# Image planes stored as 16 x 8 cells on 128 partitions, tokens by band, in a four-layer convolution kernel on one core

## The chip, the cores and the metric

One core of a Trainium2 chip runs the whole kernel in one launch. The metric is the device time of one execution in microseconds (us).

## The reference

The input is an image of 256 x 256 pixels with 128 channels, in fp32. Four layers follow each other: attention over rows, a Fourier layer with a feed-forward part, a layer of 1-D convolutions, and a gated 7 x 7 depthwise convolution. The change touches the last two. With x2 the input of the third layer, v and p its convolved values:

```
layer 3:  x3 = x2 + shift + q            (q: two ReLU'd pointwise products, added and shifted by columns)
layer 4:  n  = group_norm(x3)            (one scale and shift per channel, from statistics over the image)
          b  = conv7x7(n, B_kernel),  g = conv7x7(n, gate_B_kernel)      (per channel, periodic edges)
          bt = b * sigmoid(g)
          out = x3 + softplus(bt)-like hidden state @ W_out + b_out
```

At the 49 pixels around the origin a second kernel (A_kernel) acts as well, so those pixels are computed anew at the end.

## The kernel before, in words

The image is cut into patches of 8 x 8 pixels (PATCH); a row of patches has PX = 32 of them, and two rows of patches, 16 image rows, are a band (BAND). The stages that matter run one after another, with a barrier of all engines between them. Nearly every DMA is issued by SP, in the order written in its program; each engine works its own list in order and waits on semaphores.

**pointwise_part** (from L1301) makes x3. It has 128 tiles of two image rows, channels on partitions. A step t of the loop does, on PE, the product p_v (L1437) of tile t+1 and p_r (L1443) of tile t; on ACT, v (L1465) and r (L1477); on DVE, p (L1498), z (L1511) and, of the tile before, x3b (L1520, one instruction per image row); on POOL, q (L1415 to L1418). When a band of eight tiles is complete, it goes out in eight chunks e, nine steps after its tile: PE turns four patch columns (L1450) so that the 128 pixels of a patch column and band lie on partitions, ACT copies the result twice, into x3n (L1471) and into plane (L1481), and DVE takes statistics (L1528). SP stores x3n to the DRAM tensor x3t (L1389; "tokens"), from two buffers: ACT's copy of chunk e waits for the store of chunk e-2. After the eighth chunk POOL copies the edge columns of plane (L1423, L1424), and SP stores it to the DRAM tensor planes, in the pieces that pieces(g) lists: a band is shifted by HALO = 3 rows against the patches, so these are runs of 5, 8 and 3 rows (L1395).

```
tokens = x3t.rearrange("(g y) d a c -> g (y d) (a c)", y=BAND)
act.wait_ge(tokens_stored[e % 2], 16 * (e // 2))
```

**patch_weights** (from L1544) builds the convolution as matrices: for each group of 4 channels a [112, 2, 4, 128] block that maps a window of 14 columns x 8 rows (112 partitions, WROWS), in two halves, to 64 pixels of both convolutions. It ends with two DMAs that store them to patch_w (L1577).

**depthwise_layer** (from L1627) is the convolution and what follows it. A block b is four rows of patches; there are 8 blocks of 16 units each, 128 units u. In a unit PE turns eight slices (L1749), does two conv groups g (L1737; each 4 channels x 2 halves, reading a window and a block of weights) and one projection w = u - 6 (L1760). ACT and DVE evaluate gate and softplus (L1795 to L1813; L1857 to L1872), DVE adds the residual to the output (L1880), POOL adds a bias to the residual (L1839). Conv runs 34 groups (lead) ahead of the first turn. SP's program for unit u is: the windows of pair k = u + 17 (three DMAs, L1683), the weights of its two groups (L1689), the residual of w = u - 5 (L1695), and the four output stores of w = u - 8 (L1702), one for each image row:

```
sp.dma_start(out[0, r * PATCH + y + i].rearrange("(a d) c -> d a c", d=PATCH)[x:x + 4],
             outs[:, w % 3, i]).then_inc(stored[w % 3], 16)
```

Before them it waits: windows for the conv three pairs back, weights for the conv four groups back, the residual for `added` of w - 3, and the store for `added` of its own w.

**origin_patch** (from L1897) loads the surroundings of the origin in 27 small DMAs (L1943), and computes its 49 pixels.

## Time and profile before

| | us |
|---|---|
| median of three runs | 7585.48 (7583.73 to 7593.19) |
| the profiled execution | 7594.39 |
| its span, first to last instruction | 7592.7 |
| attention, Fourier layer and all before 4880 us | 4880, PE busy 4671 |
| pointwise stage with the statistics' end, 5080 to 5980 | 900 |
| patch weights, 5980 to 6154 | 174 |
| depthwise stage, 6154 to 7527 | 1373 |
| origin patch, 7527 to 7593 | 66 |

The profile is that of one execution. Busy is the time in which an engine executed an instruction; the DMA share is the mean over the 16 DMA engines of the core of the time in which they moved packets; GB/s is what all of them moved; PEclk is the granted TensorE clock as a share of 2.4 GHz. A wait is idle time of an engine ahead of an instruction, put down to what ended it.

### The profile page before, as it was taken

How to read it: one execution, taken by the hardware profiler on the slowest of the kernel's cores; microseconds unless marked ns; L12 is line 12 of the kernel's file. 1: busy time of each engine (PE TensorE's matmuls, PEld its weight loads, DVE VectorE, ACT ScalarE, POOL GpSimd, SP SyncE). 2: the span in 40 equal slices, each digit the busy share in tenths (PEclk: the TensorE clock that was granted, in tenths of full speed). 3: DMA queues.
4: the chain of work that ended last, by engine and by line, in shares of the span. 5: the costliest groups of instructions: out<-in, count | busy, mean ns of one | idle time of the engine just before them, and what ended most of it. 6: DMA issues, size and time to landing. Idle time of an engine off the chain costs nothing. (4 is left out here: it accounts for less than half of the span.)

```text
span 7592.7 us, 110044 instructions
## 1 busy us (share of the span) xinstructions
PE 6234.0 (82%) x29856; PEld 4091.6 (54%) x29856; DVE 3902.4 (51%) x11300; ACT 3821.1 (50%) x9727; POOL 569.5 (8%) x879
## 2 busy tenths in 40 slices
PE   7999999999999999977999899854444557777763
PEld 5777777777777776424444344311111347766663
DVE  7777777777777777413333333224444203333335
ACT  3777777777777776223444444433333203333333
POOL 0000000000000000001000000013333000111111
PEclk9999999999999999999999999987777568888886
DMA  5111111111111111673111111355444189888882
GB/s 200 34 35 35 35 34 35 35 34 34 35 35 35 34 35 41 211 230 96 59 61 56 62 59 61 107 187 164 161 156 157 52 204 207 196 195 199 196 197 70
DMA packets 759166, 773.64 MB, mean 102 GB/s; under 512 B 52640, under 2 KB 631769, under 8 KB 748121
## 3 DMA queue, kind: packets, MB, share of 16 engines
q1 hardware_dynamic: 738986, 719.10, 33.9%
q0 software_dynamic: 13312, 41.96, 1.4%
q10 hardware_dynamic: 6720, 10.76, 0.4%
q8 instruction: 75, 1.23, 0.1%
q14 instruction: 73, 0.60, 0.0%
HBM read 566.01 MB, written 205.61 MB: 102 GB/s over the span
## 5 line engine op out<-in xcount | busy, mean ns | idle before, releaser
L428 ACT ACTIVATE at_probs<-at_neg_s,at_neg_max 128x256 f32<-128x256 f32 x2048 | 1018.0, 499 | 327.1 <-DVE at_neg_max L480 320.6
L359 PE MATMUL at_p_s<-at_keys,at_qz 128*128 128x256 f32 x4096 | 1107.0, 393 | 3.2 <-ACT at_qz L453 2.5
L480 DVE CUSTOM_DVE_ANT_0 at_neg_s<-at_p_s,at_bias 128x256 f32<-128x256 f32 x2048 | 782.2, 419 | 592.7 <-PE at_p_s L359 592.6
L1737 PE MATMUL dw_p_conv<-dw_xw,dw_wts 112*128 112x128 f32 x4096 | 643.6, 323 | 412.5 <-issue 349.1
L1737 PEld LDWEIGHTS dw_p_conv<-dw_xw,dw_wts 112*128 112x128 f32 x4096 | 609.8, 235 | 433.7 <-issue 432.9
L359 PEld LDWEIGHTS at_p_s<-at_keys,at_qz 128*128 128x128 f32 x4096 | 697.7, 190 | 267.4 <-issue 209.1
L347 PE MATMUL at_p_o<-at_probs_t,at_vs 128*32 128x256 f32 x4096 | 810.0, 385 | 0.0
L492 DVE TENSOR_SCALAR at_probs<-at_probs,at_inv 128x256 f32<-128x256 f32 x2048 | 631.0, 351 | 36.2
L339 PE MATMUL at_p_t<-all_ident,at_probs 128*128 128x128 f32 x4096 | 587.1, 276 | 1.6 <-DVE at_probs_t L471 1.6
L1443 PE MATMUL pw_p_r<-pw_p,pw_w 128*128 128x512 f32 x256 | 170.4, 753 | 459.8 <-DVE pw_p L1498 459.6
L339 PEld LDWEIGHTS at_p_t<-all_ident,at_probs 128*128 128x128 f32 x4096 | 466.8, 141 | 133.1 <-issue 105.9
L1795 ACT ACTIVATE dw_gate<-dw_p_turn,dw_f_shift,dw_nscale 128x512 f32<-128x512 f32 x128 | 99.4, 777 | 792.2 <-PE dw_p_turn L1749 792.2
L935 PE MATMUL ml_p<-ml_h,l_w 128*128 128x512 f32 x1024 | 485.0, 597 | 1.6 <-DVE ml_h L1002 1.6
L347 PEld LDWEIGHTS at_p_o<-at_probs_t,at_vs 128*32 128x32 f32 x4096 | 284.7, 109 | 368.2 <-issue 128.2
L951 PE MATMUL ml_p<-ml_h,l_w1s 128*128 128x512 f32 x1024 | 469.2, 601 | 1.3 <-DVE ml_normed L1010 1.3
L1872 DVE SCALAR_TENSOR_TENSOR dw_hid<-dw_bt,dw_soft 128x512 f32<-128x512 f32 x128 | 135.2, 1057 | 592.5 <-ACT dw_soft L1813 592.5
L422 ACT ACTIVATE at_probs_t<-at_p_t 128x512 f32<-128x512 f32 x512 | 305.9, 597 | 249.6 <-PE at_p_t L339 243.3
L453 ACT ACTIVATE at_qz<-at_p_qk 32x256 f32<-32x256 f32 x1024 | 384.3, 375 | 92.0 <-PE at_p_qk L405 82.9
L981 ACT ACTIVATE ml_h<-ml_p,l_b 128x512 f32<-128x512 f32 x384 | 248.0, 679 | 282.6 <-PE ml_p L935 282.6
L428 ACT ACTIVATION_READ_ACCUMULATOR at_probs<-at_neg_s,at_neg_max 128x1 f32 x2048 | 386.2, 189 | 0.0
L1443 PEld LDWEIGHTS pw_p_r<-pw_p,pw_w 128*128 128x128 f32 x256 | 49.0, 226 | 567.5 <-DVE pw_p L1498 547.0
L471 DVE COPY at_probs_t<-at_p_t 128x512 f32<-128x512 f32 x512 | 349.3, 682 | 0.5 <-PE at_p_t L339 0.5
(214 smaller groups left out, 9837.9 us busy)
## 6 DMA issues: line engine op xcount, KB each, us to landing
dw_wts<-patch_w SPq DMA_DIRECT2D x256, 448.0 KB, 8.2
sp_xs<-x SPq DMA_DIRECT2D x256, 256.0 KB, 3.2
dw_xw<-planes SPq DMA_DIRECT2D x128, 337.5 KB
in_xs<-in_x_dram SPq DMA_DIRECT2D x32, 1024.0 KB
at_xs<-in_x_dram SPq DMA_DIRECT2D x256, 128.0 KB, 2.1
at_kvs<-in_L_conv_kv_x_dram SPq DMA_DIRECT2D x256, 128.0 KB, 2.3
x<-at_x1s SPq DMA_DIRECT2D x256, 128.0 KB, 1.9
ml_xs<-x SPq DMA_DIRECT2D x128, 256.0 KB
```

Of the source, the lines that this page charges most:

```text
L339: mm = pe.transpose(p_t[h % 2][:, kh, qh * 128:(qh + 1) * 128], probs[:, h, qh, kh * 128:(kh + 1) * 128], ident[:, :])
L347: mm = pe.matmul(p_o[ch, 0, :], vs[:, row.r % 2, kh, ch], probs_t[:, h, kh, :], start=kh == 0, stop=kh == HALVES - 1)
L359: mm = pe.matmul(p_s[h % 2][:, qh, :], qz[:, row.r % 2, h, qh * 128:(qh + 1) * 128], keys[:, row.r, h // 2, :], start=True, stop=True)
L422: act.activation(probs_t[:, h], p_t[h % 2][:, :, :], ACT.Copy).then_inc(odd_read, 1)
L428: e = act.activation(probs[:, h, qh, :], neg_s[:, h % 2, qh, :], ACT.Exp, bias=neg_max[:, row.r % 2, i:i + 1], scale=-1.0, accum_out=sums[ ...
L453: t = act.activation(qz[ch, two.r % 2, h, :], p_qk[ch, 0, :], ACT.Copy, scale=float(HEAD_DIM) ** -0.5)
L471: dve.tensor_copy(probs_t[:, h], p_t[h % 2][:, :, :]).then_inc(even_read, 1)
L480: t = dve.tensor_tensor_reduce(neg_s[:, h % 2, qh, :], p_s[h % 2][:, qh, :], bias[:, h, qh, :], -1.0, 3.0e38, ALU.add, ALU.min, neg_max[:, ...
L492: t = dve.tensor_scalar(probs[:, h, qh, :], probs[:, h, qh, :], inv[:, p, j:j + 1], None, ALU.mult)
L935: pe.matmul(p_1[b][:, :], w0[:, b * 128:(b + 1) * 128], h[:, :], start=True, stop=True).then_inc(hid_made, 1)
L951: mm = pe.matmul(p_2[:, :], w1c[:, b, :], h1[:, b, :], start=b == 0, stop=b == blocks - 1)
L1737: mm = pe.matmul(p_conv[g % 2][:, j, :], wts[:, g % 4, half, j, :], xw[:, k % 3, half:half + BLOCK_PY, g % 2 * 4 + j, 0:PX], start=half == ...
```

## The change

The planes are kept as cells of 16 rows x 8 columns: the DRAM tensor planes has 264 image rows, 8 columns d, 128 channels and 33 patch columns (WIDE), shifted by four columns (SHIFT), so that a window is 128 partitions of one DMA and the second half of a window is the next patch column (side) instead of the next patch row. The weights have 128 partitions. x3b gets a 33rd column of patches and is written in four instructions per tile instead of two; POOL copies its first column's edge (x3_wrapped), and PE and DVE wait for that. x3t is ordered by band, patch column, pixel of the band. Tokens have four buffers; the planes of a band go out in eight DMAs, one a step, from 18 steps behind the tile, with an edge DMA in the first and in the last band. In the depthwise stage residual and output are four DMAs each of 32 partitions x 4 rows; they have four buffers, the residual is loaded one unit later and the output stored two units later in SP's order.

```diff
-WIDE = PX + 2
-PATCH_ROWS = ROWS // PATCH + 1
+WIDE = PX + 1
+SHIFT = PATCH // 2
...
-    tokens = x3t.rearrange("(g y) d a c -> g (y d) (a c)", y=BAND)
+    tokens = x3t[:, :, 0:128].rearrange("g a p c -> g p a c")
...
-        x3b = m.sb("x3b", [128, 2, PX, BAND, PATCH])
-        x3n = m.sb("x3n", [128, 2, 4, CH])
+        x3b = m.sb("x3b", [128, 2, PX + 1, BAND, PATCH])
+        x3n = m.sb("x3n", [128, 4, 4, CH])
...
-        tokens_stored = [m.sem(f"tokens_stored{i}") for i in range(2)]
+        tokens_stored = [m.sem(f"tokens_stored{i}") for i in range(4)]
...
-        steps = range(-2, tiles + 12)
...
+        steps = range(-2, tiles + 20)
+        bands = ROWS // BAND
+        edge = SHIFT * PATCH
+        first_row = planes[0:SHIFT].rearrange("y d c a -> (y d) (c a)")
+        last_row = planes[ROWS + SHIFT:ROWS + 2 * SHIFT].rearrange("y d c a -> (y d) (c a)")
+        body = planes[SHIFT:ROWS + SHIFT].rearrange("(g y) d c a -> g (y d) (c a)", y=BAND)
+        part = CH * WIDE // 8
+
+        def token_stores(e):
+
+            return 16 * (e // 4) + (16 * len(range(0, e, 8)) if e % 4 == 0 else 0)
 
         def plane_stores(parity, g):
 
-            return 16 * sum(len(pieces(k)) for k in range(parity, g, 2))
+            return 16 * 8 * len(range(parity, g, 2)) + (16 if parity == 0 and g > 0 else 0) + (16 if g == bands and parity else 0)
 
         @block.sync
...
-                    sp.dma_start(tokens[e // 8][:, e % 8 * 4 * CH:(e % 8 + 1) * 4 * CH],
-                                 x3n[:, e % 2].rearrange("p a c -> p (a c)")).then_inc(tokens_stored[e % 2], 16)
-                if e >= 0 and e % 8 == 7:
-                    g = e // 8
-                    sp.wait_ge(plane_wrapped, g + 1)
-                    for y, n, r_at, y_at in pieces(g):
-                        sp.dma_start(planes[r_at, :, y_at:y_at + n].rearrange("d y c a -> y d (c a)"),
-                                     plane[y * PATCH:(y + n) * PATCH, g % 2].rearrange("p c a -> p (c a)")
-                                     ).then_inc(planes_stored[g % 2], 16)
+                    sp.dma_start(tokens[e // 8][:, e % 8 * 4:(e % 8 + 1) * 4], x3n[:, e % 4]).then_inc(tokens_stored[e % 4], 16)
+                    if e % 8 == 0:
+                        sp.dma_start(tokens[e // 8][:, PX], x3n[:, 0, 0]).then_inc(tokens_stored[0], 16)
+                f = t - 18
+                if 0 <= f < chunks:
+                    g, k = f // 8, f % 8
+                    flat = plane[:, g % 2].rearrange("p c a -> p (c a)")
+                    if k == 0:
+                        sp.wait_ge(plane_wrapped, g + 1)
+                    sp.dma_start(body[g][:, k * part:(k + 1) * part], flat[:, k * part:(k + 1) * part]
+                                 ).then_inc(planes_stored[g % 2], 16)
+                    if k == 7 and g == 0:
+                        sp.dma_start(last_row, flat[0:edge]).then_inc(planes_stored[0], 16)
+                    if k == 7 and g == bands - 1:
+                        sp.dma_start(first_row, flat[128 - edge:128]).then_inc(planes_stored[1], 16)
+            for s in range(4):
+                sp.wait_ge(tokens_stored[s], token_stores(chunks + s))
             for s in range(2):
-                sp.wait_ge(tokens_stored[s], 16 * (chunks // 2))
-                sp.wait_ge(planes_stored[s], plane_stores(s, ROWS // BAND))
+                sp.wait_ge(planes_stored[s], plane_stores(s, bands))
...
+                if 0 <= t - 8 < tiles and t % 8 == 0:
+                    g = t // 8 - 1
+                    pool.wait_ge(x3_made, 8 * g + 8)
+                    pool.tensor_copy(x3b[:, g % 2, 0, :, 0:SHIFT], x3b[:, g % 2, PX, :, 0:SHIFT]).then_inc(x3_wrapped, 1)
...
-                    pool.tensor_copy(plane[:, g % 2, :, 0:1], plane[:, g % 2, :, PX:PX + 1])
-                    pool.tensor_copy(plane[:, g % 2, :, PX + 1:PX + 2], plane[:, g % 2, :, 1:2]).then_inc(plane_wrapped, 1)
+                    pool.tensor_copy(plane[:, g % 2, :, PX:PX + 1], plane[:, g % 2, :, 0:1]).then_inc(plane_wrapped, 1)
...
                     pe.wait_ge(x3_made, 8 * g + 8)
+                    pe.wait_ge(x3_wrapped, g + 1)
...
-                    if e >= 2:
-                        act.wait_ge(tokens_stored[e % 2], 16 * (e // 2))
-                    act.activation(x3n[:, e % 2], p_n[e % 2][:, :, :], ACT.Copy).then_inc(tokens_read, 1)
+                    if e >= 4:
+                        act.wait_ge(tokens_stored[e % 4], token_stores(e))
+                    act.activation(x3n[:, e % 4], p_n[e % 2][:, :, :], ACT.Copy).then_inc(tokens_read, 1)
...
-                    act.activation(plane[:, g % 2, :, 1 + px:5 + px], p_n[e % 2][:, :, :].rearrange("p a c -> p c a"),
+                    act.activation(plane[:, g % 2, :, px:px + 4], p_n[e % 2][:, :, :].rearrange("p a c -> p c a"),
                                    ACT.Copy).then_inc(plane_read, 1)
...
                     for i in range(2):
-                        x3 = dve.scalar_tensor_tensor(out=x3b[:, g % 2, :, y + i, :],
-                                                      in0=xs[:, y + 1 + i].rearrange("p (a d) -> p a d", d=PATCH), scalar=shift,
-                                                      in1=q[:, s, i].rearrange("p (a d) -> p a d", d=PATCH),
-                                                      op0=ALU.add, op1=ALU.add)
+                        for d, a_at in ((0, 1), (SHIFT, 0)):
+                            cols = slice(SHIFT - d, 2 * SHIFT - d)
+                            x3 = dve.scalar_tensor_tensor(
+                                out=x3b[:, g % 2, a_at:a_at + PX, y + i, d:d + SHIFT],
+                                in0=xs[:, y + 1 + i].rearrange("p (a d) -> p a d", d=PATCH)[:, :, cols], scalar=shift,
+                                in1=q[:, s, i].rearrange("p (a d) -> p a d", d=PATCH)[:, :, cols], op0=ALU.add, op1=ALU.add)
                     x3.then_inc(x3_made, 1)
...
                     dve.wait_ge(x3_made, 8 * g + 8)
+                    dve.wait_ge(x3_wrapped, g + 1)
...
-        sel = m.sb("sel", [KTAPS, 2 * PATCH, PATCH - 1 + WINDOW, PATCH])
+        sel = m.sb("sel", [KTAPS, BAND, PATCH - 1 + BAND, PATCH])
         kt = m.sb("kt", [KTAPS, 2, CH])
-        tw = m.sb("tw", [WROWS, 2, CH, 2 * SPOTS])
+        tw = m.sb("tw", [128, 2, CH, 2 * SPOTS])
...
                     mm = pe.matmul(p_w[n % 4][:, i].rearrange("p f c -> p (f c)"),
-                                   sel[:, first, PATCH - 1 - ox:PATCH - 1 - ox + WINDOW, :].rearrange("t a b -> t (a b)"),
+                                   sel[:, half * PATCH - ox + PATCH - 1, PATCH - 1 - oy:PATCH - 1 - oy + BAND, :].rearrange("t a b -> t (a b)"),
                                    kt[:, :, :].rearrange("p f c -> p (f c)"), start=True, stop=True)
...
-        xw = m.sb("xw", [WROWS, 3, BLOCK_PY + 1, 8, WIDE])
-        wts = m.sb("wts", [WROWS, 4, 2, 4, 2 * SPOTS])
+        xw = m.sb("xw", [128, 3, BLOCK_PY, 8, WIDE])
+        wts = m.sb("wts", [128, 4, 2, 4, 2 * SPOTS])
...
-        xr = m.sb("xr", [128, 3, 4, CH])
-        outs = m.sb("outs", [128, 3, 4, CH])
+        xr = m.sb("xr", [128, 4, 4, CH])
+        outs = m.sb("outs", [128, 4, 4, CH])
...
         flat = xw[:, :, :, :, :].rearrange("p k r c a -> p k r (c a)")
-        run = 8 * WIDE - 2
+        run = 8 * WIDE
         cell = CH * WIDE
 
-        def field(r, d, y, c, col, planes_of):
-
-            at = ((r * PATCH + d) * PATCH + y) * cell + c * WIDE + col
-            return bass.AP(planes.tensor, at, [[cell, planes_of * PATCH], [PATCH * PATCH * cell, BLOCK_PY + 1], [1, run]])
+        def windows(b, c):
+
+            at = b * BLOCK_PY * PATCH * PATCH * cell + c * WIDE
+            return bass.AP(planes.tensor, at, [[cell, 128], [PATCH * PATCH * cell, BLOCK_PY], [1, run]])
...
-                for d, n, at, col in ((PATCH - HALO, HALO, 0, 0), (0, PATCH, HALO, 1), (0, HALO, HALO + PATCH, 2)):
-                    sp.dma_start(flat[at * PATCH:(at + n) * PATCH, k % 3, :, 0:run],
-                                 field(b * BLOCK_PY, d, 0, c, col, n)).then_inc(x_loaded[k % 3], 16)
+                sp.dma_start(flat[:, k % 3], windows(b, c)).then_inc(x_loaded[k % 3], 16)
...
             def load_residual(w):
-                r, x, y = w // 4, w // 2 % 2 * 4, w % 2 * 4
-                if w >= 3:
-                    sp.wait_ge(added, w - 2)
-                sp.dma_start(xr[:, w % 3],
-                             x3t[r * PATCH + y:r * PATCH + y + 4, x:x + 4].rearrange("y d a c -> (d a) y c")).then_inc(r_loaded[w % 3], 16)
+                r, x, y = w // 4, w // 2 % 2, w % 2 * 4
+                if w >= 4:
+                    sp.wait_ge(added, w - 3)
+                cells = x3t[r // 2, x:x + PX, r % 2 * 64:r % 2 * 64 + 64].rearrange("a (y d) c -> d a y c", d=PATCH)
+                for d in range(4):
+                    sp.dma_start(xr[d * PX:(d + 1) * PX, w % 4], cells[(1 - x) * SHIFT + d][:, y:y + 4]).then_inc(r_loaded[w % 4], 16)
 
             def store(w):
                 r, x, y = w // 4, w // 2 % 2 * 4, w % 2 * 4
                 sp.wait_ge(added, w + 1)
-                for i in range(4):
-                    sp.dma_start(out[0, r * PATCH + y + i].rearrange("(a d) c -> d a c", d=PATCH)[x:x + 4],
-                                 outs[:, w % 3, i]).then_inc(stored[w % 3], 16)
+                for d in range(4):
+                    sp.dma_start(out[0, r * PATCH + y:r * PATCH + y + 4].rearrange("y (a d) c -> d a y c", d=PATCH)[x + d],
+                                 outs[d * PX:(d + 1) * PX, w % 4]).then_inc(stored[w % 4], 16)
...
-                if 0 <= u - 5 < total:
-                    load_residual(u - 5)
-                if 0 <= u - 8 < total:
-                    store(u - 8)
-            for s in range(3):
-                sp.wait_ge(stored[s], 64 * ((total - s + 2) // 3))
+                if 0 <= u - 6 < total:
+                    load_residual(u - 6)
+                if 0 <= u - 10 < total:
+                    store(u - 10)
+            for s in range(4):
+                sp.wait_ge(stored[s], 64 * (total // 4))
...
-                    pe.wait_ge(x_loaded[k % 3], 48 * (k // 3 + 1))
+                    pe.wait_ge(x_loaded[k % 3], 16 * (k // 3 + 1))
...
-                    for half in range(2):
-                        mm = pe.matmul(p_conv[g % 2][:, j, :], wts[:, g % 4, half, j, :],
-                                       xw[:, k % 3, half:half + BLOCK_PY, g % 2 * 4 + j, 0:PX],
-                                       start=half == 0, stop=half == 1)
+                    for side in range(2):
+                        mm = pe.matmul(p_conv[g % 2][:, j, :], wts[:, g % 4, side, j, :],
+                                       xw[:, k % 3, :, g % 2 * 4 + j, side:side + PX], start=side == 0, stop=side == 1)
...
-                pool.wait_ge(r_loaded[w % 3], 16 * (w // 3 + 1))
-                pool.tensor_tensor(xr[:, w % 3], xr[:, w % 3], b_plain.unsqueeze(1).broadcast_to((128, 4, CH)),
+                pool.wait_ge(r_loaded[w % 4], 64 * (w // 4 + 1))
+                pool.tensor_tensor(xr[:, w % 4], xr[:, w % 4], b_plain.unsqueeze(1).broadcast_to((128, 4, CH)),
...
-                if w >= 3:
-                    dve.wait_ge(stored[w % 3], 64 * (w // 3))
-                dve.tensor_tensor(outs[:, w % 3], p_out[w % 2][:, :, :], xr[:, w % 3], ALU.add).then_inc(added, 1)
+                if w >= 4:
+                    dve.wait_ge(stored[w % 4], 64 * (w // 4))
+                dve.tensor_tensor(outs[:, w % 4], p_out[w % 2][:, :, :], xr[:, w % 4], ALU.add).then_inc(added, 1)
...
-                k = min(left, 128 - at % 128)
-                pieces.append((at, y, x, k))
+                k = min(left, 128 - at % 128, PATCH - (x + SHIFT) % PATCH)
+                pieces.append((at, y, x + SHIFT, k))
...
+        def cells(y, x, k):
+
+            first = y % BAND * PATCH + x % PATCH
+            return x3t[y // BAND, x // PATCH, first:first + k]
...
-                sp.dma_start(xs[at % 128:at % 128 + k, at // 128, :], x3t[y, x % PATCH:x % PATCH + k, x // PATCH]).then_inc(loaded, 16)
+                sp.dma_start(xs[at % 128:at % 128 + k, at // 128, :], cells(y, x, k)).then_inc(loaded, 16)
...
-    x3t = scratch("x3t", [ROWS, PATCH, PX, CH])
-    planes = scratch("planes", [PATCH_ROWS, PATCH, PATCH, CH, WIDE])
+    x3t = scratch("x3t", [ROWS // BAND, WIDE, BAND * PATCH + 1, CH])
+    planes = scratch("planes", [ROWS + 2 * SHIFT, PATCH, CH, WIDE])
```

## Rows read from the trace of the kernel before

**Rows 1.** Busy by stage: us, each engine, granted clock, DMA share, GB/s
```profile
5080.00:5980.00 900.00, 372.01 (x1030) 168.29 (x1030) 408.59 (x648) 299.30 (x513) 288.97 (x544) 0.73 0.47 155
6300.00:7500.00 1200.00, 850.82 (x5446) 831.48 (x5447) 437.79 (x608) 422.37 (x738) 159.19 (x124) 0.82 0.82 190
```

**Rows 2.** Waits, 5090 to 5940 us: total, times, longest
```profile
DVE pw_x3b L1520 <- POOL pw_q L1418: 421.2, 80, 28.9
ACT pw_x3n L1471 <- DMA x3t<-pw_x3n: 371.7, 16, 29.3
```

**Rows 3.** Busy by short stretch, columns as in rows 1
```profile
5916.00:5933.00 17.00, 0.00 (x0) 0.00 (x0) 0.28 (x1) 0.00 (x0) 0.00 (x0) 0.50 0.34 125
7522.00:7526.00 4.00, 0.00 (x0) 0.00 (x0) 0.00 (x0) 0.00 (x0) 0.00 (x0) 0.50 0.25 75
6180.00:6270.00 90.00, 68.33 (x430) 66.05 (x430) 9.68 (x14) 7.77 (x13) 0.00 (x0) 0.77 1.02 221
20.00:60.00 40.00, 31.17 (x256) 27.48 (x254) 38.91 (x65) 0.00 (x0) 0.00 (x0) 1.00 1.01 415
3250.00:3350.00 100.00, 84.62 (x188) 18.58 (x186) 0.00 (x0) 28.18 (x48) 0.00 (x0) 1.00 0.83 267
```

**Rows 4.** Timeline, 5360 to 5385 us: start, us, engine, line
```profile
5361.59 0.88 DVE L1520 SCALAR_TENSOR_TENSOR pw_x3b<-pw_xs,all_coef,pw_q 128x256 f32<-128x256 f32 x2 [2.28 <-POOL pw_q L1418]
...
5363.58 1.66 DVE L1511 SCALAR_TENSOR_TENSOR pw_z<-pw_xs,all_coef,pw_taus 128x512 f32<-128x512 f32 x1
...
5376.48 1.17 DVE L1520 SCALAR_TENSOR_TENSOR pw_x3b<-pw_xs,all_coef,pw_q 128x256 f32<-128x256 f32 x2
```

**Rows 5.** Timeline, end of the pointwise stage
```profile
5934.74 0.60 ACT L1471 ACTIVATE pw_x3n<-pw_p_n 128x512 f32<-128x512 f32 x1 [20.34 <-DMA x3t<-pw_x3n]
...
5944.77 6.01 SPq L1395 DMA_DIRECT2D planes<-pw_plane  x4
5973.85 3.62 DVE L173 BATCH_NORM_AGGREGATE l_gn_mv<-stats 128x2 f32<-128x768 f32 x1 [57.58 <-PEq L77]
```

**Rows 6.** Tile pw_xs: ns min/median/max, first and last start
```profile
L1520 DVE SCALAR_TENSOR_TENSOR pw_x3b<-pw_xs,all_coef,pw_q x256: 471/483/1462, 5093.5 to 5910.3; 128x256 f32<-128x256 f32 x128
```

**Rows 7.** DMA issues, 6400 to 7500 us: KB each, us to landing
```profile
dw_wts<-patch_w SPq DMA_DIRECT2D x192, 448.0 KB, 8.2
dw_xw<-planes SPq DMA_DIRECT2D x96, 337.5 KB
...
dw_xr<-x3t SPq DMA_DIRECT2D x115, 256.0 KB, 7.2
dw_xw<-planes SPq DMA_DIRECT2D x192, 126.6 KB
```

**Rows 8.** Tile dw_p_turn: ns min/median/max, first and last start
```profile
L1749 PE MATMUL dw_p_turn<-all_ident,dw_raw x1024: 273/310/421, 6280.1 to 7489.2; 128*128 128x128 f32 x171
```

**Rows 9.** Timeline, one unit of the depthwise stage
```profile
6805.07 5.52 SPq L1702 DMA_DIRECT2D out_dram<-dw_outs  x4
...
6809.72 2.02 PE L1737 MATMUL dw_p_conv<-dw_xw,dw_wts 112*128 112x128 f32 x16 [2.04 <-issue]
...
6811.58 1.05 PE L1760 MATMUL dw_p_out<-all_w_plain,dw_hid 128*128 128x128 f32 x8
...
6814.26 1.33 PE L1749 MATMUL dw_p_turn<-all_ident,dw_raw 128*128 128x128 f32 x8
```

**Rows 10.** Busy in two stretches, columns as in rows 1
```profile
6500.00:6700.00 200.00, 143.20 (x927) 140.14 (x926) 67.88 (x97) 65.14 (x114) 24.66 (x19) 0.83 0.85 197
4880.00:5028.00 148.00, 116.72 (x258) 20.98 (x258) 0.34 (x2) 62.67 (x32) 0.00 (x0) 0.97 0.70 242
```

**Rows 11.** Timeline, the store of the patch weights and the next stage
```profile
6100.00 15.12 SPq L1577 DMA_DIRECT2D patch_w<-kw_tw  x2
6154.36 1.04 SPq L1683 DMA_DIRECT2D dw_xw<-planes  x2
```

**Rows 12.** Tile og_xs: ns min/median/max, first and last start
```profile
L1943 SPq DMA_DIRECT2D og_xs<-x3t x27: 258/296/300, 7527.3 to 7536.1; - x27
```

More of the change, by code:

```diff
@@ L1534 @@
 SPOTS = PATCH * PATCH
-WROWS = PATCH * WINDOW
 BLOCK_PY = 4
@@ L1559, in patch_weights @@
         p_t = m.ps("p_t", [KTAPS, 2, CH])
-        p_w = [m.ps(f"p_w{i}", [WROWS, 2, 2, CH]) for i in range(4)]
+        p_w = [m.ps(f"p_w{i}", [128, 2, 2, CH]) for i in range(4)]
         p_b = m.ps("p_b", [128, CH])
@@ L1658, in depthwise_layer @@
         w_loaded = [m.sem(f"w_loaded{i}") for i in range(4)]
-        r_loaded = [m.sem(f"r_loaded{i}") for i in range(3)]
-        stored = [m.sem(f"stored{i}") for i in range(3)]
+        r_loaded = [m.sem(f"r_loaded{i}") for i in range(4)]
+        stored = [m.sem(f"stored{i}") for i in range(4)]
         scaled, prepared, biased = m.sem("scaled"), m.sem("prepared"), m.sem("biased")
@@ L1712, in _ @@
                 load_weights(2 * k + 1)
-            for u in range(total + 8):
+            for u in range(total + 10):
                 k = u + lead // 2
@@ L2075, in build @@
     tau = scratch("tau", [TOKENS])
-    patch_w = scratch("patch_w", [CH // 4, WROWS, 2, 4, 2 * SPOTS])
+    patch_w = scratch("patch_w", [CH // 4, 128, 2, 4, 2 * SPOTS])
     with ExitStack() as ctx:
```

29 lines of the change are left out of this document (7 added, 22 removed).

## The prediction

> **What bounds the kernel now.** I read the busy shares by stage first, then the waits, then short stretches with only one kind of transfer in flight, then timelines of one tile and one unit.
>
> The pointwise stage lasts 900 us, and no engine is busy for half of it: DVE 409, PE 372, ACT 299 us [rows 1]. The waits give the reason: ACT stands 371.7 us in 16 waits, one per band, for the token store to leave its buffer [rows 2], 23.2 us each. DVE's 421 us behind POOL's q is the same wait further down the chain. During such a wait (5916 to 5933) the DMA share is 0.34 at 125 GB/s [rows 3]: transfers are outstanding, yet two thirds of the DMA engines rest. What is outstanding is a burst: the band's planes go out in DMAs of 5, 8 and 3 rows (680, 1088, 408 KB), 17,408 bytes to a packet, and the token stores queue behind them. At the stage's end the burst runs alone, from its issue at 5944.8 to the next stage's first work at 5973.9 [rows 5].
>
> The depthwise stage is about 1370 us. Per unit PE does 48 matmul records (32 conv, 8 turn, 8 project); 927 in 200 us [rows 10] are 19.3 units, so a unit takes 10.35 us. I use 10.3. PE is busy 72% of it, at clock 0.83, and its idle time stands before the first conv of a unit (2.04 us in this one [rows 9]), with no releaser but its loads. SP spends 5.52 us on the four output stores [rows 9], though an issue costs 0.52 us (two in 1.04 [rows 11]); the rest is waiting for room in the queue. When only stores are left (7522 to 7526) the DMA share is 0.25 at 75 GB/s [rows 3]: a store occupies four engines of sixteen. Those four are the bound. A unit moves 591 KB windows, 896 KB weights and 256 KB each of residual and of output (four stores of 64 KB) [rows 7]. Windows and weights, 1.52 MB at the 221 GB/s of the lead phase (share 1.02 [rows 3]), take 6.9 us; 0.26 MB of output at 75 GB/s takes 3.5 us on four engines; the sum, 10.4, is a unit.
>
> The Trainium skill (DMA: Bandwidth & Descriptors, section "Why a DMA increments its semaphore by 16 and not by 1") says that a DMA runs on the largest number of engines up to 16 that divides the slowest dimension of both sides. By it the old output stores (DRAM side 4 x 32) run on 4, the plane pieces on 5, 8 and 3, the old side windows (24 partitions) on 12, and every new form of these on 16. The trace agrees for the stores (share 0.25); for the other forms no row isolates it.
>
> **Pointwise stage, part by part.** The plane burst becomes eight DMAs per band, one per tile, each over 128 partitions with 2,112 bytes, issued a band later. Tokens get four buffers instead of two. So nothing large stands ahead of a token store, and I take all 16 waits away. Next late is DVE. Between waits, x3 starts at 5361.59 and four tiles later at 5376.48 [rows 4]: 3.72 us per tile.
>
> Added: x3 is made by four instructions of 128 elements instead of two of 256. A 512-element one takes 0.74 us [rows 4], a 256-element one 0.48 [rows 6], so 128 elements are some 0.35 us: 4 x 0.35 - 2 x 0.48 = +0.44 us, less the overlap that makes a pair 0.88 [rows 4]; I take +0.33. Below: 0, since DVE also waits here for POOL (2.28 us [rows 4]); above: 2 x 0.48 = +0.97. So 4.05 us per tile, bounds 3.7 and 4.7. From 5093.5 to 5910.3 [rows 6], 817 us, it becomes 127 x 4.05 = 514: **-303 us** (-347 to -220).
>
> At nothing: the new POOL copy of x3's edge, once a band (one plane copy goes, and POOL is busy 289 of 900 us); PE and DVE's wait for it comes a tile later; the token store's 512 packets of 512 bytes in place of 128 of 2,048, with the same bytes. A tile moves 1.07 MB. At the 267 GB/s and share 0.83 of a stretch with loads and stores together [rows 3], that is 322 GB/s at full share and 3.3 us, below 4.05. If that cover went, 221 GB/s would give 4.8 us per tile (+95 us). SP issues four or five DMAs a tile, 2.1 to 2.6 us at 0.52. ACT's wait for planes two bands back now ends with a part issued in the same step; the step's length covers it, or it costs up to 2 us in 14 bands.
>
> The end: from the last x3 at 5910.3 to 5973.9 is 63.5 us, 20.3 of it a token wait and 29 the last burst [rows 5]. Then: eight chunks at about 1.2 us, 10; the POOL copy, 1; 2.2 MB of planes and the 0.5 MB edge at 322 GB/s, 8; landing and step lags, 5. Together 24: **-39 us**.
>
> **Patch weights.** 112 partitions become 128: bytes +14%. The store takes 54.4 us from issue to the next stage [rows 11]: +7.8 at the same rate; at 415 GB/s the 16.8 MB are 40 us, -14. The first row is nearer; I take **+3 us**. Matmuls move as many columns as before.
>
> **Depthwise stage.** Windows: one DMA of 528 KB for three; weights 1024 KB for 896. The lead phase loads 17 pairs between its first load at 6154.4 [rows 11], plus 8 us to land, and the first turn at 6280.1 [rows 8]: 118 us, 6.9 us each. 1.59 MB at 322 GB/s are 4.9 us, at 221 7.2. I take 5.1: **-31 us** (-45 to +5).
>
> A unit then moves 2.11 MB on all engines: 6.6 us at 322, 5.1 at 415, 9.6 at 221 GB/s. I take 322, since that row mixes loads and stores as a unit does. PE needs 2 x 2.02 + 1.05 + 1.33 = 6.4 us [rows 9]; a stretch busy for 79% was granted 0.97 [rows 10], so 6.6. Two limits of 6.6 us that don't stay in step give some 0.7 us on top: 7.3, bounds 6.5 and 8.0. DVE (68 us in 19.3 units) and ACT (65) need 3.5. SP issues 11 DMAs instead of 10, 5.7 us at 0.52. For 110 units: 3.0 x 110 = **-330 us**.
>
> That the new stores and residual loads use all engines is a choice between two rows: the form with 4 outermost on the DRAM side ran at share 0.25, the loads with 24 to 128 outermost at share 1.0 [rows 3]; the new ones have 32 outermost on both sides. The moved store: it now waits for an output three steps old, so SP does not stand there, and the next unit's windows and weights behind it in SP's queue are not held. The residual load comes one unit later; it is needed about two units (15 us) on, against 7.2 us to landing [rows 7] and POOL's 1.3. If that cover went, DVE would wait with its next raw copy behind it. The last 17 units have no loads and run on the ACT-DVE chain: 0 (-10 to +5).
>
> **Origin patch.** 53 load DMAs instead of 27. 27 take 8.8 us in a row [rows 12], 0.34 each: 26 x 0.34 = **+9 us**, exposed.
>
> **Sum.** -303 - 39 + 3 - 31 - 330 + 9 = -691. The profiled execution took 7594.4 us: 6903. It stands 9 us over the median of the three runs, so 6895.
>
> **Rivals.**
> *The 32-partition transfers run at half rate.* Residual and output, four DMAs of 32 partitions each, are 0.52 MB, 1.6 us at 322 GB/s; twice that makes a unit 8.9 us: 6895 + 176 = 7070. For: no row has such a form. Against: four such DMAs can be in flight together.
> The Trainium skill (SBUF — State Buffer, section "Door 1: The DMA port swizzle") has the rule that speaks for it: 32 or 64 partitions reach only half of the SBUF's DMA ports. No run here shows it yet.
>
> *The windows and weights are slow for their own sake.* The lead phase had all engines busy and still 221 GB/s. If that rate holds, a unit takes 9.6 us and the lead gains nothing: 6895 + 253 + 36 = 7184. For: share 1.02. Against: 415 GB/s over 128 partitions [rows 3], and the new transfers are over 128.
>
> *A new wait keeps half of ACT's.* If planes and tokens in turns still hold a token buffer or the plane wait for 11.6 us a band: 6895 + 186 = 7081. Against: the share was 0.34 during the waits, so room is there.
>
> *Stores stay on a quarter of the engines* (the change does not do it): a unit keeps 10.3: 7225.
>
> *Slower:* the residual, on all engines now, falls to a quarter too, since it is split in four. Then four engines carry 0.52 MB at 75 GB/s, 7.0 us, beside 1.59 MB at 221, 7.2: a unit of 14.2 us, +3.9 x 110 = 429 over before, lead +5. 7585 - 342 + 429 + 5 + 12 = 7689. It decides from a unit of 13.3 us on, where it eats the pointwise gain. Against: both sides of these DMAs have 32 outermost.
>
> **How the numbers follow.** Forecast 0.54, own range 6760 to 7060. Half rate 0.13, 221 GB/s 0.16, new wait 0.10, quarter stays 0.02, slower 0.04, no change 0.01. The range 6740 to 7220 takes all cases but the last three. A measurement tells 0.2% (15 us) from none. Faster 0.95, same 0.01, slower 0.04.
>
> **What would show it.** The ACT wait for token stores near 0; the pointwise stage near 558 us; x3 every 4.05 us with 0.35 us instructions; depthwise units of 7.3 us with PE at 0.95 or more; the four stores on SP about 2 us; the share at the stage's end well over 0.25; the lead near 87 us; the origin loads 18 us. It is wrong if units stay over 9 us, if the DMA share is 1.0 at about 220 GB/s, or if x3 needs over 4.7 us.

## The result and the profile after

Before 7588.18 us (median of 4 runs on the same chip), after **6764.64 us** (4 runs, 6757.97 to 6768.1): ratio 0.8913, 95% interval 0.8898 to 0.8929. Forecast 6895, range 6740 to 7220. The profiled execution took 6757.97 us, its span is 6756.3 (before: 7592.7). The 836.4 us between the two spans, cut at the same events in both traces (differences are taken before rounding):

| stretch | before | after | difference | forecast |
|---|---|---|---|---|
| pointwise, first x3 to the aggregate behind the stage | 880.4 | 533.2 | -347.2 | -342 |
| store of the patch weights, issue to the next stage | 54.4 | 45.8 | -8.5 | +3 |
| depthwise, first load to first turn (lead) | 125.7 | 77.8 | -48.0 | -31 |
| 110 units, first turn to last conv | 1130.6 | 697.3 | -433.3 | -330 |
| the last 17 units | 116.6 | 105.7 | -10.9 | 0 |
| origin patch | 65.4 | 72.9 | +7.5 | +9 |
| ahead of the first x3, and between aggregate and that store | | | +4.0 | 0 |

Busy by stage after, columns as in [rows 1] (the pointwise stage, the lead phase, 200 us of units, the last units):

```profile
5084.00:5640.00 556.00, 364.74 (x1029) 158.93 (x1029) 467.96 (x906) 296.54 (x513) 297.04 (x544) 0.89 0.83 252
5820.00:5870.00 50.00, 45.65 (x386) 43.72 (x385) 8.30 (x12) 7.16 (x12) 0.00 (x0) 1.00 1.03 384
6100.00:6300.00 200.00, 183.51 (x1500) 178.48 (x1499) 115.95 (x160) 106.95 (x187) 46.63 (x31) 1.00 1.08 334
6577.00:6683.00 106.00, 59.01 (x329) 54.79 (x328) 63.87 (x81) 53.01 (x90) 31.53 (x24) 0.76 0.47 121
```

In the pointwise stage the share of the transfers went from 0.47 [rows 1] to 0.83 and DVE is busy 84% of the time. The lead phase loads at 384 GB/s instead of 221 [rows 3] with the same full engines, which points to the forms of the transfers; the second group of experiments tests that. In the units TensorE went from 0.83 of its clock at 72% busy [rows 10] to 1.00, its level of 2.4 GHz, at 92% busy.

The waits of the pointwise stage after (total, times, longest):

```profile
DVE pw_x3b L1527 <- POOL pw_q L1419: 50.3, 80, 2.0
ACT pw_plane L1486 <- DMA planes<-pw_plane: 18.5, 13, 3.1
ACT pw_x3n L1476 <- DMA x3t<-pw_x3n: 0.7, 3, 0.2
```

The 371.7 us of [rows 2] are 0.7. The prediction's "up to 2 us in 14 bands" for ACT's wait on the planes is the second line: 13 waits of 1.4 us in the mean, the longest 3.1. The instructions of x3, of the convolution (in the fifth line that of before) and of the turn, first and last start, and the origin patch's loads:

```profile
L1527 DVE SCALAR_TENSOR_TENSOR pw_x3b<-pw_xs,all_coef,pw_q x512: 336/347/1309, 5096.9 to 5603.0; 128x128 f32<-128x128 f32 x171
L1742 PE MATMUL dw_p_conv<-dw_xw,dw_wts x4096: 270/273/550, 5808.0 to 6577.7; 128*128 128x128 f32 x196
L1753 PE MATMUL dw_p_turn<-all_ident,dw_raw x1024: 276/310/421, 5880.4 to 6651.6; 128*128 128x128 f32 x171
L1952 SPq DMA_DIRECT2D og_xs<-x3t x53: 242/256/296, 6683.4 to 6699.6; - x53
L1737 PE MATMUL dw_p_conv<-dw_xw,dw_wts x4096: 270/275/555, 6162.3 to 7410.7; 112*128 112x128 f32 x196
```

x3: (5603.0 - 5096.9) / 127 = 3.99 us a tile [rows 6: 6.43]. Units: (6577.7 - 5880.4) / 110 = 6.34 us; before, with [rows 8] and the fifth line, (7410.7 - 6280.1) / 110 = 10.28. This stretch holds the convolutions of units 0 to 110, which is nearly 111 units, so the figure is a little high: from the first turn of unit 0 to that of unit 110 the traces have 6.28 us a unit after and 10.16 before. Every unit below is worked out in the same way, by 110, and is about 1% too long; the comparisons stand. The timeline of one unit after (start, us, engine, line):

```profile
6203.59 2.02 PE L1742 MATMUL dw_p_conv<-dw_xw,dw_wts 128*128 128x128 f32 x16 [0.78 <-issue]
...
6206.34 1.95 PE L1742 MATMUL dw_p_conv<-dw_xw,dw_wts 128*128 128x128 f32 x16
6206.56 1.90 SPq L1707 DMA_DIRECT2D out_dram<-dw_outs  x4
...
6208.51 0.48 SPq L1688 DMA_DIRECT2D dw_xw<-planes  x1
6209.04 1.16 SPq L1693 DMA_DIRECT2D dw_wts<-patch_w  x2
...
6210.24 2.43 SPq L1701 DMA_DIRECT2D dw_xr<-x3t  x4
6210.27 2.02 PE L1742 MATMUL dw_p_conv<-dw_xw,dw_wts 128*128 128x128 f32 x16 [0.81 <-issue]
```

The four stores take 1.90 us where they took 5.52 [rows 9]. TensorE still rests 0.8 us ahead of the first conv, and SyncE issues all the time: 0.48 + 1.16 + 2.43 + 1.90 is 5.97 us of 6.34. Three things could bound it, TensorE, SyncE and the transfers; the third and fourth group of experiments ask which.

### The profile page after: what moved, and what is told of

The parts are those of the page before. It is cut to its first block and busy times, and to the rows that moved or that the text cites. A ratio compares the mean times of both kernels' runs of the same rounds, so it can differ in the third digit from the quotient of the medians.

```text
span 6756.3 us, 110680 instructions
## 1 busy us (share of the span) xinstructions
PE 6036.4 (89%) x29856; PEld 3901.5 (58%) x29856; DVE 3969.5 (59%) x11556; ACT 3817.0 (56%) x9727; POOL 606.3 (9%) x879
## 5 line engine op out<-in xcount | busy, mean ns | idle before, releaser
L1742 PE MATMUL dw_p_conv<-dw_xw,dw_wts 128*128 128x128 f32 x4096 | 507.9, 276 | 109.7 <-DMA dw_wts<-patch_w 55.2
L1742 PEld LDWEIGHTS dw_p_conv<-dw_xw,dw_wts 128*128 128x128 f32 x4096 | 479.1, 190 | 128.4 <-issue 127.4
L1876 DVE SCALAR_TENSOR_TENSOR dw_hid<-dw_bt,dw_soft 128x512 f32<-128x512 f32 x128 | 155.8, 1217 | 320.8 <-ACT dw_soft L1817 320.7
L935 PEld LDWEIGHTS ml_p<-ml_h,l_w 128*128 128x128 f32 x1024 | 195.7, 191 | 250.6 <-issue 245.9
L1010 DVE SCALAR_TENSOR_TENSOR ml_normed<-ml_p,l_vec,ml_rstd 128x512 f32<-128x512 f32 x128 | 96.1, 751 | 410.0 <-ACT ml_rstd L975 410.0
L707 POOL DMA_DIRECT2D mixed<-mx_gs x64 | 34.6, 542 | 3353.1 <-DVE mx_gs L767 3348.3
```

The source lines that it names most:

```text
L935: pe.matmul(p_1[b][:, :], w0[:, b * 128:(b + 1) * 128], h[:, :], start=True, stop=True).then_inc(hid_made, 1)
L1742: mm = pe.matmul(p_conv[g % 2][:, j, :], wts[:, g % 4, side, j, :], xw[:, k % 3, :, g % 2 * 4 + j, side:side + PX], start=side == 0, stop= ...
```

## The experiments

Each is the kernel after (or before, where said) with one edit. Each was measured beside the kernel before on the same chip, which had medians of 7586 to 7588 us.

### Old stores in the new kernel, new stores in the old one

```diff
-for d in range(4): sp.dma_start(out[...]"y (a d) c -> d a y c"[x + d], outs[d * PX:(d + 1) * PX, w % 4])
+for i in range(4): sp.dma_start(out[0, r * PATCH + y + i]"(a d) c -> d a c"[x:x + 4], outs[:, w % 4, i])
```

> The changed kernel with the four output stores of a unit in the old form (one image row each, 128 partitions, 4 outermost on the DRAM side). Theory (the form decides how many DMA engines a store occupies): the stores take about 3.0 to 3.5 us on four engines beside 1.59 MB at some 380 GB/s (4.2 us) and the residual (0.7 us), so a depthwise unit goes from 6.3 to 7.9 to 8.4 us, the kernel to 6935 to 6990 us, and SP stands several us in its stores again. Rival (storing two units later removed the stall): the unit stays at 6.3 us and the kernel at 6765 us.

Measured: 6957.68 us, ratio 0.917 (0.9143 to 0.9196). First turn 5881.2, last conv 6771.1: 8.09 us a unit, and the lead phase is untouched (378 GB/s). The stretch of units and SyncE's timeline:

```profile
6100.00:6300.00 200.00, 159.46 (x1182) 155.71 (x1181) 89.35 (x123) 83.42 (x146) 32.38 (x24) 0.92 0.84 259
```

```profile
6199.62 3.94 SPq L1707 DMA_DIRECT2D out_dram<-dw_outs  x4
```

Share 0.84 with stores that stand 3.94 us in the queue. If four engines are busy all the time, the other twelve are busy for (16 x 0.84 - 4) / 12 = 0.79 of it (an estimate; the trace has no share of a single engine). The form of the stores alone is worth 193 us in the new kernel. Now the same edit the other way, the only one made to the kernel before:

> The kernel before with only the output stores in the new form (32 partitions x 4 rows, four DMAs); layout, buffers and order as before. Theory (two separate causes: stores on four engines, and windows and weights at 221 GB/s): the unit moves 2.05 MB at 221 GB/s, 9.3 us instead of 10.3, the kernel 7475 us. Rival (the four engines are the whole of it, the slow loads were their consequence): the unit falls to 7 us or less, the kernel to 7200 us or less.

Measured: 7403.67 us, ratio 0.9757 (0.9729 to 0.9786); (7238.0 - 6284.4) / 110 = 8.67 us a unit. The theory had 9.3: it used the lead phase's 221 GB/s, and the units ran at 238 with share 1.03:

```profile
6500.00:6700.00 200.00, 155.60 (x1115) 152.19 (x1114) 83.45 (x115) 78.86 (x138) 30.88 (x23) 0.89 1.03 238
```

So the stores' form was the first bound of the old kernel (10.3 us a unit). Behind it, at 8.7, the share says that all engines were full at a low rate; but SyncE also stands still for a good part of this unit (see the moved stores below), and these runs don't separate the two.

### Which form makes the bytes dear: windows or weights

Weights in the old partition split (112, here with the other 16 in a second DMA), and windows in three DMAs of 24, 64 and 40 partitions (24, 64 and 24 in the kernel before); the rest of each kernel is after's.

```diff
-sp.dma_start(wts[:, g % 4], patch_w[g % groups])
+sp.dma_start(wts[0:112, g % 4], patch_w[g % groups][0:112])
+sp.dma_start(wts[112:128, g % 4], patch_w[g % groups][112:128])
```

> The changed kernel with each weight load cut into DMAs of 112 and 16 partitions, same bytes. Theory A (112 partitions over 16 engines, 7 each, is a slow form): the lead phase falls from 384 GB/s to under 300 and its pairs from 4.1 to 5.5 us or more, units to 8 us, the kernel to 6950 us or more. Theory B (the windows in 24, 64 and 24 partitions were the slow form): the lead phase keeps over 350 GB/s; the two more issues of SP per unit (0.8 us) cost up to 0.8 us a unit, the kernel 6765 to 6850 us.

```diff
-sp.dma_start(flat[:, k % 3], windows(b, c))
+for first, n in ((0, 24), (24, 64), (88, 40)):
+    sp.dma_start(flat[first:first + n, k % 3], windows(b, c, first, n))
```

> The changed kernel with each window load cut into DMAs of 24, 64 and 40 partitions, same bytes. Theory B (those forms were the slow ones in the kernel before): the lead phase falls from 384 GB/s to 250 to 300, its pairs to 5.5 us or more, units to 8 us, the kernel to 6950 us or more. Theory A (the 112 partitions of the weights were): the lead keeps over 350 GB/s, and two more issues of SP cost up to 0.9 us a unit, the kernel 6765 to 6860 us.

Measured, one run each: 7023.37 and 7041.59 us, units of (6842.5 - 5919.9) / 110 = 8.39 and (6861.5 - 5919.2) / 110 = 8.57 us. The lead phase and the units of the first, then of the second:

```profile
5820.00:5870.00 50.00, 34.43 (x255) 32.49 (x254) 5.54 (x8) 4.78 (x8) 0.00 (x0) 0.93 1.07 254
6100.00:6300.00 200.00, 158.74 (x1152) 154.86 (x1152) 89.84 (x119) 80.45 (x141) 31.23 (x24) 0.91 1.08 253
```

```profile
5820.00:5870.00 50.00, 33.33 (x241) 31.14 (x242) 5.06 (x8) 4.18 (x7) 0.00 (x0) 0.93 1.01 248
6100.00:6300.00 200.00, 158.69 (x1149) 155.13 (x1148) 88.05 (x117) 82.07 (x144) 30.31 (x23) 0.90 1.00 251
```

Each theory expected its own form to be the culprit, and each form alone brings every load from 384 down to about 250 GB/s, at a full share. The weights, unchanged in the second kernel, had packets of 4096 bytes that took 247 ns in the lead phase and 230 in the units (means over the trace's packets) where after has 167 and 175; in the first kernel the unchanged windows took 72 ns for 1056 bytes in the lead phase where after has 49. A transfer in the bad form slows its neighbours. The first kernel adds a DMA of 16 partitions besides the 112, and that DMA alone was not tried. Seven of eight of its 4096-byte packets belong to the 112 partitions; their median in the lead phase is 272 ns, and in the kernel before, which has no DMA of 16 partitions but the windows in three, it is 268. Whether the number of partitions, the one at which a DMA starts (0, 24, 88) or the number of engines it gets makes these forms slow, the runs don't tell apart.

### What bounds a unit now: TensorE, SyncE or the bytes

One kernel leaves out half of the convolution's matmuls, one half of the weights' bytes (both matmuls use the first half):

```diff
-for side in range(2): mm = pe.matmul(p_conv[...], wts[:, g % 4, side, j, :], ..., start=side == 0, stop=side == 1)
+mm = pe.matmul(p_conv[...], wts[:, g % 4, 0, j, :], ..., start=True, stop=True)
```

> The kernel after, with the second of the two matmuls of each channel of the convolution (side 1) left out; every load and store stays. In the kernel after a unit takes 6.34 us, TensorE is busy 92% of it and the transfers stand at a share of 1.07 and 334 GB/s. If the transfers (or SyncE, which issues them) bound the unit: unit 6.1 to 6.35 us, share 1.07, total 6740 to 6770 us, TensorE's busy share near 0.6. If TensorE bounds it: the convolution is over half of its 5.8 us, so the unit falls until the transfers stop it, at 5.5 to 6.0 us, the rate rises to 350 GB/s or more, total 6665 to 6725 us.

```diff
-sp.dma_start(wts[:, g % 4], patch_w[g % groups])
+sp.dma_start(wts[:, g % 4], patch_w[g % groups][:, 0])
```

> The kernel after, with only the first half of each group's weights loaded (256 KB for 512) and used by both matmuls; TensorE's work, the number of transfers and SyncE's issues stay. If the transfers' volume bounds the unit: it falls from 6.34 us to what TensorE needs, 5.8 to 6.0 us, total 6695 to 6730 us, and the share falls under 0.9. If TensorE (with its idle 0.8 us once a unit) or SyncE's issues bound it: unit 6.25 to 6.35 us, total 6745 to 6770 us; SyncE's busy time in the unit then tells which: full if it is SyncE, under 5.5 us if TensorE.

Measured, one run each: 6753.31 and 6691.24 us. Units of the first, then of the second:

```profile
6100.00:6300.00 200.00, 149.15 (x1005) 142.72 (x1005) 120.56 (x156) 106.25 (x187) 44.57 (x31) 0.90 1.07 331
```

```profile
6100.00:6300.00 200.00, 196.82 (x1650) 195.50 (x1649) 123.08 (x174) 116.65 (x205) 44.44 (x34) 1.00 1.01 275
```

With a third of TensorE's matmuls gone (busy 149 us in 200 for 184, at a granted clock of 0.90 for 1.00) a unit still takes (6574.9 - 5880.5) / 110 = 6.31 us at 331 GB/s: not TensorE. With 256 KB less for each group and the same 11 DMAs it takes (6509.6 - 5866.8) / 110 = 5.84 us and TensorE is busy 98% of the time: not SyncE's issues, and 5.84 us is what TensorE needs. What the transfers carry bounds the unit, by half a microsecond over TensorE. (The second line's share is 1.01 at 275 GB/s, although TensorE is the bound there: a share near 1 does not by itself say that the transfers are the bound.)

### The moved stores

```diff
-load_residual(u - 6) ... store(u - 10)
+load_residual(u - 5) ... store(u - 8)
```

> The kernel after, with the residual loads and the stores back at their old places in SyncE's order (5 and 8 units behind, not 6 and 10); the four buffers stay. My theory, in which the move is worth nothing: 6745 to 6785 us, ratio to the kernel after 1.00. A rival, in which SyncE waits on each store for the addition and holds up the loads behind it: the unit gains 0.3 us or more, total 6800 us or more, with a wait of SyncE on VectorE's addition in the depthwise stage of over 0.2 us a unit.

Measured: 6857.69 us (4 runs, 6842.52 to 6865.56), ratio 0.9044 (0.9027 to 0.9062). My theory fell, the rival was right and the move is worth 93 us. In the profiled run a unit took (6660.6 - 5877.6) / 110 = 7.12 us. The wait is that of the store: the residual loads still have their fourth buffer and show none. SyncE's waits in 200 us of that kernel, and its stretch:

```profile
SPq L1707 <- DVE dw_outs L1884: 31.0, 22, 3.6
SPq L1693 <- PE dw_p_conv L1742: 3.1, 5, 1.8
SPq L1688 <- PE dw_p_conv L1742: 0.4, 1, 0.4
```

```profile
6100.00:6300.00 200.00, 172.39 (x1345) 167.67 (x1345) 103.70 (x141) 96.02 (x168) 39.18 (x28) 0.96 0.99 299
```

28 units in these 200 us: SyncE stands 1.1 us a unit for the addition that the store needs, the next windows and weights behind it, and the rate falls to 299 GB/s. After has no such line (its waits in all 700 us of units are 33.1 and 10.6 us for conv and 3.6 for the residual's buffer). Before and the second experiment have a wait for the same addition in the old order, at the residual load:

```profile
SPq L1695 <- DVE dw_outs L1880: 21.1, 19, 2.6
```

```profile
SPq L1695 <- DVE dw_outs L1880: 116.5, 33, 5.8
```

(before in 6500 to 6700, the old kernel with new stores in 6400 to 6700.) With three buffers, residual load u-5 waits for addition u-8, the very one for which store u-8 waits. Once the stores no longer filled the queue, SyncE stood here 3.4 us a unit. So in the old kernel I moved the store:

```diff
-outs, stored: 3 buffers; store(u - 8)
+outs, stored: 4 buffers; store(u - 10)
```

> The kernel before with the new form of the output stores, now issued 10 units behind instead of 8, with four output buffers; residual loads, windows and weights as before, in their old forms and order. With the stores alone at their old place the unit was 8.67 us and SyncE stood 100.6 us in 300 on VectorE's addition. If that wait costs here what it costs in the kernel after (93 us between the two orders): unit 7.9 us, total about 7310 us. If the old windows and weights are the bound at 238 to 254 GB/s whatever SyncE does: 2.0 MB a unit are 8.0 to 8.5 us, total 7320 to 7390 us with no wait of SyncE left; the share (1.03 already with the stores at their old place) speaks for the upper end.

Measured: 7409.8 us (7403.74 to 7415.86), no gain over 7403.67. Neither case is decided by it, since SyncE's wait stayed (in 6400 to 6700):

```profile
SPq L1695 <- DVE dw_outs L1880: 120.0, 33, 5.6
```

The residual load still had three buffers and its old place. So in the old kernel the store's place alone is worth nothing. With a fourth residual buffer as well that kernel does not fit into SBUF (its last tensor needs 8192 bytes a partition, 7488 are left), so what both are worth beside the old windows and weights was not measured, nor was what either is worth without the other in the new kernel.

### The pointwise stage: buffers and split x3

```diff
-x3n, tokens_stored: 4 buffers
+x3n, tokens_stored: 2 buffers
```

> The kernel after with two token buffers in place of four; the planes still go out in eight parts a band. Theory: the burst of planes ahead of the token stores was the whole of ScalarE's 371 us, so splitting it is enough: total 6755 to 6785 us, ScalarE's wait for token stores under 20 us. Rival: the buffers are needed as much as the split, since a token store now stands in the queue behind a plane part and two loads: a wait of 0.5 us or more a tile, total 6830 us or more.

Measured: 6759.93 us (6754.27 to 6765.59). ACT's wait for token stores:

```profile
ACT pw_x3n L1476 <- DMA x3t<-pw_x3n: 6.9, 8, 1.6
```

The two added buffers bring nothing in the total: 6759.93 us is inside after's range. What took away the 371 us is the rest of the change. The order of SyncE's program points to the burst of planes that stood ahead of the tokens, but the planes were split, issued later and given 128 partitions in place of 40, 64 and 24 all at once, and the tokens got another layout; no run tells these apart.

```diff
-for d, a_at in ((0, 1), (SHIFT, 0)): x3 = dve.scalar_tensor_tensor(out=x3b[..., a_at:a_at + PX, y + i, d:d + SHIFT], ...)
+x3 = dve.scalar_tensor_tensor(out=x3b[:, g % 2, 1:PX + 1, y + i, :], ...)
```

> The kernel after, with x3 written by two additions a tile of 512 elements over whole cells, as before, in place of four of 256; the image stands four columns off in the cells, so the output is that of a shifted layout. All else stays. From the rows, four take 4 x 0.347 = 1.39 us busy of VectorE but 1.14 us end to end, two of 512 took 2 x 0.48 = 0.97 us. Theory, VectorE's chain sets the pointwise stage at 3.99 us a tile: saves 0.2 to 0.3 us a tile, 25 to 38 us, total 6725 to 6740 us. Rival, another engine's hand-over sets it: total 6755 to 6770 us.

Measured: 6736.72 us (6735.49 to 6737.95), 28 us less (2 runs; the slowest is 20 us below after's fastest). Besides the additions, POOL's copy of the edge takes whole cells of 8 columns for 4.

```profile
L1525 DVE SCALAR_TENSOR_TENSOR pw_x3b<-pw_xs,all_coef,pw_q x256: 470/482/1399, 5101.4 to 5585.9; 128x256 f32<-128x256 f32 x128
```

(5585.9 - 5101.4) / 127 = 3.81 us a tile against 3.99: the split in four costs 0.18 us a tile, a third of what VectorE's busy time says (467.96 against 401.96 us, 0.52 a tile). The rest comes out of its wait for POOL's q, 50.3 us in 80 waits after and 99.6 us in 81 here, so VectorE is not alone in setting the pace.

### Is it the short packets?

The unit's rate is 334 GB/s, the lead phase's 384. A unit has 512 KB in runs of 512 bytes, the lead has none. Numbering a patch's spots by column gives stores and residual loads runs of 2048 bytes, and one DMA for four stores:

```diff
-oy, ox = divmod(spot + i, PATCH)
+ox, oy = divmod(spot + i, PATCH)
-spot = (y + i) * PATCH + x
+spot = (x + i) * PATCH + y
-for d in range(4): store "y (a d) c -> d a y c"[x + d] from outs[d * PX:(d + 1) * PX, w % 4]
+store "y (a d) c -> (y a) d c"[:, x:x + 4] from outs[:, w % 4]
```

> The kernel after with the 64 spots of a patch numbered column by column, so that an output tile holds 4 rows x 32 patches on its partitions and 4 neighbouring tokens in each: a store is one DMA over 128 partitions with runs of 2048 bytes in place of four with 512, and the four residual loads have runs of 2048 bytes; bytes, TensorE's work and results are the same. If the 512-byte packets are what holds a unit's transfers at 334 GB/s where the lead phase, with long packets alone, has 384: 2.11 MB take 5.5 us, TensorE's 5.9 us (measured with half the weights) becomes the bound, unit 5.9 to 6.0 us, total 6715 to 6730 us. If the mixture of reads and writes is what costs: unit 6.3 us, total 6755 to 6770 us.

Measured: 6760.63 us (4 runs, 6753.81 to 6772.77): no gain.

```profile
6100.00:6300.00 200.00, 185.35 (x1512) 180.04 (x1512) 127.57 (x160) 108.01 (x189) 46.35 (x31) 1.00 1.05 333
```

```profile
SPq L1693 <- PE dw_p_conv L1741: 76.1, 49, 2.3
```

333 GB/s as before it. SyncE now has time left over and spends it, 76 us in 200, on waiting for a free weights buffer, which once more rules it out as the bound. The packets of residual and output did get cheaper, 100 ns for 2048 bytes where four of 512 took 4 x 35 = 140, but those of the weights rose from 175 to 195 ns and those of the windows from 52 to 57 (means over 6100 to 6300), so whatever sets the rate passed the gain on. Neither run length nor number of DMAs holds the rate at 334. Two explanations are left over and not told apart: that reads and writes together cost it, and the residual loads, which still go over 32 partitions each.

### A version with less

The last group of weights stays in SBUF, a residual buffer goes for it, and the origin patch's loads are issued from two queues:

```diff
+if g >= groups and g % groups in kept: return    # load_weights, kept = (31,)
-xr: 4 buffers
+xr: 3 buffers
-for at, y, x, k in pieces: sp.dma_start(...)
+for at, y, x, k in pieces[0::2]: sp.dma_start(...)
+for at, y, x, k in pieces[1::2]: act.dma_start(...)
```

> The kernel after with two things cut: of the 32 groups of weights the last one stays in SBUF after its first load (7 of 256 loads of 512 KB less, 3.7 MB; the room comes from a fourth residual buffer, which goes), and the origin patch's 53 loads are issued from SyncE's and ScalarE's queues in turn. If a unit is bound by its bytes: 3.7 MB at 334 GB/s are 11 us less; the loads of the origin patch take 8 us for 16.5: total 6740 to 6750 us. If the third residual buffer is too few, the units give it back: 6755 us or more.

Measured: 6750.1 us (5 runs, 6745.39 to 6750.84), ratio to before 0.8895 (0.8883 to 0.8907); after's is 0.8913 (0.8898 to 0.8929), and these intervals overlap, though the slowest of the five runs is 7 us below after's fastest.

```profile
L1964 SPq DMA_DIRECT2D og_xs<-x3t x27: 240/272/293, 6684.1 to 6692.3; - x27
L1997 ACTq DMA_DIRECT2D og_xs<-x3t x26: 256/293/372, 6684.1 to 6692.1; - x26
```

The loads end after 8.2 us for 16.2, and the origin patch from its first load to the end takes 65.0 us for 72.9: that part came. The kept group did not: (6572.3 - 5873.6) / 110 = 6.35 us a unit. In 5880 to 6580 SyncE waits at the residual load for the addition for 19.9 us in 24 waits (after: 3.6 in 9), and the rate is 321 GB/s for 329. So the third buffer has a price. Whether it is all of the missing 11 us, or a unit is not so simply bound by its bytes, stays open.

## Why the prediction was right, and where its terms were off

**The order of things was right.** The ACT waits went, VectorE's chain was next, the stores went to all engines (their old form in the new kernel costs 193 us), the windows and weights got faster, and no large new wait took over.

**Pointwise stage, -303 and -39, measured -311 and -37.** x3's pace is 3.99 us for 4.05. The share of +0.33 for the split was 0.18, the base 3.81 for 3.72; that the pace came out so near is in part luck, since the two misses cancel. From the last x3 to the aggregate it is 5603.0 to 5630.1, 27 us for 24. The two extra token buffers, named beside the planes as if both did it, had no part in the total.

**Depthwise units, -330, measured -433: the term that was mis-sized.** Three steps are in it. The rate of 322 GB/s was near (334, so 6.3 us for 6.6). TensorE's need, added up to 6.4 and set to 6.6 from rows whose instructions overlap, is 5.84. And "two limits of 6.6 us that don't stay in step give some 0.7 us on top" had no row behind it: measured, a unit takes what its bytes take, with TensorE half a microsecond below. The added 0.7 is most of the difference between 7.3 and 6.34, and the limit of 6.6 the rest; 0.96 us in 110 units are 106 us, of the 130 by which the forecast was too high.

**The unit before, 6.9 + 3.5 = 10.4 us.** The prediction added 6.9 us of windows and weights and 3.5 us of stores to the time of a unit. The sum leaves out the 256 KB of residual, and takes the stores and the loads one after the other. With the stores on all engines and all else as before, the unit fell by 1.6 us, to 8.67. That the stores' form came first was right; that the sum met 10.3 does not show its terms.

**The moved stores, priced at nothing.** The prediction said that SyncE does not stand there, which is so, but only of the new place; back at the old one, the wait for the addition costs 93 us. That before already waited for this addition, 21.1 us in 200 at the residual load, the prediction does not mention. Without the move the forecast of 7.3 us would have been met for a wrong reason: 7.12.

**Lead phase, -31, measured -48.** 4.1 us a pair for 5.1: (77.8 - 8) / 17, since the loads alone ran at 384 GB/s, between the 322 I took and the 415 of another stretch.

**Patch weights, +3, measured -8.5.** The lower bound of -14 was nearer. The old store had 112 partitions as well, and I had taken its rate as if the form did not matter: 14.7 MB in 54.4 us are 270 GB/s, 16.8 MB in 45.8 are 366. That the form is the reason was not tested for stores.

**Last units and origin patch.** -10.9 for 0, just past the bound of -10; +7.5 for +9, at 0.31 us a load for 0.34.

**The rivals.** Half rate for 32 partitions did not come: the unit moves 512 KB that way and still runs at 334 GB/s. The Trainium skill's rule (SBUF — State Buffer, "Door 1") that 32 partitions reach half of the ports did not show as a price here: with other transfers in flight, one store over 128 partitions in place of four over 32 changed nothing (6761 for 6765 us). Alone such a DMA was not measured. 221 GB/s for its own sake was the rival with most weight (0.16), and the experiments on windows and weights show why it fell: the low rate came with the old forms, and the change removed both. With a form like one of them left it is 7023 or 7042 us. The new-wait case was met in small: 18.5 us at the planes, not 186. That the stores stay on a quarter of the engines, or that the residual joins them there, is refuted by the unit of 6.34 us and by the first experiment, where only the old form costs 8.09.

## What to carry to other kernels

Look at the partition count of every load that shares the queues: one stream of 112 and 16, or of 24, 64 and 40, partitions took all loads from 384 to about 250 GB/s, so padding to 128 paid although the weights have 14% more bytes. A share of 1.0 at a low rate points to the form, if no engine is the bound; a share of 0.25 says that few of the DMA engines work. And when a slow transfer is made fast, follow its queue to the next wait: here, a store behind an unfinished addition would have kept 93 us.

## What the runs showed of the hardware

- Transfers over 24, 64 and 40 partitions slow others beside them: 4096-byte packets of unchanged weights loads took 247 and 230 ns for 167 and 175 (lead phase and units).
- Loads alone ran at 384 GB/s, loads and stores together, in units that TensorE doesn't bound, at 329 to 336, with runs of 512 bytes as with runs of 2048 (334 and 333).
- A share of 1.01 stood beside a stretch that TensorE bounded, at 275 GB/s.
